# Key path ahead of the queries, squares' low part on GpSimd and the kernel's small constant folded into the context product, in an eight-batch attention and expert kernel

## The reference, cut to what matters

```python
def softmax_kernel(x, proj, is_query):        # 16 heads of 16, proj is 64 x 16
    xp = einsum('bhnd,md->bhnm', x * norm, proj)
    diag = sum(square(x), -1) * 0.5 * norm * norm
    stab = max(xp, -1) if is_query else max(xp, (-1, -2))
    return ratio * (exp(xp - diag - stab) + EPS_K)
qp, kp = softmax_kernel(q, ..., True), softmax_kernel(k, ..., False)
k_sum = sum(kp, 2);  denom = einsum('bhnm,bhm->bhn', qp, k_sum)
ctx = einsum('bhnm,bhnd->bhmd', kp, v)
out = einsum('bhnm,bhmd->bhnd', qp, ctx) / denom
```

## Time and profile before

| | us |
|---|---|
| median of three runs | 785.72 (785.5 to 789.7) |
| the profiled execution's own time | 786.12 |
| its span, first to last instruction | 784.4 |
| TensorE busy | 728.6 (93%) |
| VectorE busy | 619.0 (79%) |
| ScalarE busy | 469.6 (60%) |
| GpSimd busy | 375.3 (48%) |
| mean granted TensorE clock, of full speed | 0.977 |

### The profile page before, as it was taken

One profiled execution on the slowest core, in us unless ns is written; L12 is line 12 of the kernel. 1 busy time (PEld: TensorE's weight loads), 2 busy tenths in 40 slices (PEclk: granted clock), 3 DMA queues, 4 the chain that ended last, 5 costly groups with the idle time before them and its releaser, 6 DMA issues. The chain is left out here.

```text
span 784.4 us, 16225 instructions
## 1 busy us (share of the span) xinstructions
PE 728.6 (93%) x6009; PEld 597.0 (76%) x6009; DVE 619.0 (79%) x1304; ACT 469.6 (60%) x749; POOL 375.3 (48%) x358
## 2 busy tenths in 40 slices
PE   8999999999999999999999979968999999999950
PEld 7867768778778778778778758857888889998850
DVE  5976678888888888888888797888768767778683
ACT  4656747867867867867868834463245544455470
POOL 4364317527527527527617613511347556544563
PEclk9999999999999999999999999999999999999985
DMA  8100010011011011011011011250336664446593
GB/s 252 33 2 2 1 54 2 28 54 57 28 53 54 27 53 54 27 53 54 27 54 29 29 55 54 60 193 2 124 134 163 160 165 112 107 148 168 138 266 112
DMA packets 51184, 62.60 MB, mean 80 GB/s; under 512 B 9408, under 2 KB 44992, under 8 KB 51136
## 3 DMA queue, kind: packets, MB, share of 16 engines
q1 hardware_dynamic: 44016, 49.74, 19.3%
q0 software_dynamic: 6864, 12.19, 7.9%
q10 hardware_dynamic: 256, 0.03, 0.0%
HBM read 40.85 MB, written 21.10 MB: 79 GB/s over the span
## 5 line engine op out<-in xcount | busy, mean ns | idle before, releaser
L2181 PE MATMUL pF<-w,h 128*128 128x256 f32 x448 | 109.8, 386 | 0.0
L2181 PEld LDWEIGHTS pF<-w,h 128*128 128x128 f32 x448 | 80.7, 190 | 17.6 <-issue 8.6
L1139 POOL DMA_INDIRECT kp<-row_scratch,idx_g x32 | 43.3, 1353 | 76.5 <-DVE idx_g L1851 53.5
L904 ACT ACTIVATE h<-pX,b1cur 128x512 f32<-128x512 f32 x64 | 43.9, 689 | 56.4 <-DVE b1cur L1954 41.8
L2636 PE MATMUL pX<-w_lo,h_hi 128*128 128x256 f32 x256 | 73.9, 289 | 0.8 <-issue 0.8
L2636 PE MATMUL pX<-w_hi,h_lo 128*128 128x256 f32 x256 | 72.4, 283 | 0.0
L2636 PE MATMUL pX<-w_hi,h_hi 128*128 128x256 f32 x256 | 72.4, 283 | 0.0
L993 POOL TENSOR_SCALAR ve<-mv 128x4 f32<-128x4 f32 x36 | 8.5, 237 | 133.2 <-DVE mv L1216 132.3
L1147 POOL DMA_INDIRECT acc_scratch<-qp,idx_s x28 | 55.5, 1982 | 21.5 <-DVE qp L1891 16.6
L1912 DVE TENSOR_TENSOR h_lo<-h,h_hi 128x512 fp32r<-128x512 f32 x64 | 42.5, 690 | 22.9 <-ACT h_hi L896 22.2
L1321 DVE RECIPROCAL den<-den 128x512 f32<-128x512 f32 x14 | 46.9, 3348 | 7.9 <-ACT den L551 7.9
(11 more groups left out here) (435 smaller groups left out, 2165.6 us busy)
## 6 DMA issues: line engine op xcount, KB each, us to landing
kp<-fc1T SPq DMA_DIRECT2D x8, 1024.0 KB
w<-fc2T SPq DMA_DIRECT2D x8, 1024.0 KB
xin<-video SPq DMA_DIRECT2D x7, 512.0 KB, 3.5
x<-video SPq DMA_DIRECT2D x7, 512.0 KB, 4.5
out<-x SPq DMA_DIRECT2D x7, 512.0 KB, 3.0
acc_scratch<-xf SPq DMA_DIRECT2D x7, 512.0 KB, 2.9
row_scratch<-y SPq DMA_DIRECT2D x7, 512.0 KB, 3.0
kp<-acc_scratch SPq DMA_DIRECT2D x4, 512.0 KB, 5.8
```

Source lines behind the costliest of these rows:

```text
L904: nc.scalar.activation(h[:, n, :], pM[n % M_SLOTS], ACT.Gelu_apprx_tanh, bias=b1cur[:, n:n + 1]).then_inc(he_ready, 1)
L1139: pool.indirect_dma_start(xg[:, g, :], None, row_d, bass.IndirectOffsetOnAxis(ap=idx_g[:, g:g + 1], axis=0)).then_inc(first_rows[g] if isi ...
L2181: ins = nc.tensor.matmul(pF[m][:, half * D:(half + 1) * D], h[:, k, tok(2 * m + half)], w2[:, k, :], start=(k == 0), stop=(k == FC - 1))
```

## The change

It does the following.

- **Order on TensorE, batches 2 to 7:** `key_features(0)` goes ahead of the values, `key_features(1)` ahead of the first `hidden`; `turn_kmax` comes after three `hidden` steps (before: six), `spread_kmax` after five (before: seven), the second query features after six (before: seven). `ff_out` is handed out in counts: 2, turn_tops, 6, context, features_turned(0), 4, sums_of_keys, features_turned(1), turn_context, 4, all_heads, 5, transposes of xf, 3, gates, 3, turn_x, turn_gates, 5. Batch 1 keeps its early keys and has the same rest.
- **VectorE:** both first `k_max` stand ahead of the low part of x2T, `k_top` ahead of the first two `q_max`; `rest_of_squares` is gone from batches 1 to 7; the statistics of the next batch and `scores` stand ahead of `residual`; `add_ff(0)` behind `sums_of_context`; the gates' copy behind both `heads_out`.
- **ScalarE:** `eps_k` is gone; the exp of the key tiles goes between the last relus, the norms of z behind them, `cs_copy(0)` ahead of `exp_q(0)`; xf's norm behind `dens`; `normed_rows` to the end.
- **GpSimd:** runs `rest_of_squares` behind the two passes over x2; the ksum adds wait for all four `k_sub`; `xnb` goes to the end of the batch.
- **EPS_K:** the key tile gets two more columns of EPS_K behind each pair of 128 (stride 130). `context` multiplies 129 columns, so that the last one is EPS_K times the sum of the values; `cs_copy(0)` copies that column out and adds it as a bias, `cs_copy(1)` adds 512 times EPS_K. The extra products of batch 0 are gone.
- `ones_h` and `sdiag` have 128 rows (before 16). On SyncE the DMA of the scores comes one batch later, behind that of y.

```diff
@@ ScalarE
             def cs_copy(i, n):
                 act.wait_ge(a_ready, i * A_JOBS + J_CTX + n + 1)
-                nc.scalar.activation(cs[:, n, :], pA[n][:, 0:G * P], ACT.Copy).then_inc(cs_ready, 1)
+                if n:
+                    nc.scalar.activation(cs[:, 1, :], pA[1][:, 0:G * P], ACT.Identity, bias=epsn_c[:, 0:1]).then_inc(cs_ready, 1)
+                else:
+                    wide = pA[0][:, 0:G * PW].rearrange("p (g x) -> p g x", x=PW)
+                    nc.scalar.activation(vsum[:].unsqueeze(2), wide[:, :, P:P + 1], ACT.Copy).then_inc(vsum_ready, 1)
+                    act.wait_ge(vsum_ready, i + 1)
+                    for g in range(G):
+                        ins = nc.scalar.activation(cs[:, 0, g * P:(g + 1) * P], wide[:, g, 0:P], ACT.Identity, bias=vsum[:, g:g + 1])
+                    ins.then_inc(cs_ready, 1)
...
-            def eps_k(i, t):
-                act.wait_ge(ke_ready, (i - 1) * TT + t + 1)
-                nc.scalar.activation(kp[:, t, :], kp[:, t, :], ACT.Identity, bias=epsk_c[:, 0:1]).then_inc(kp_ready, 1)
...
@@ GpSimd
+            def rest_of_squares(i):
+
+                pool.wait_ge(qsq_ready, (i + 1) * 2)
+                pool.wait_ge(x_ready, (i - 1) * X_JOBS + J_QT + 2)
+                nc.gpsimd.tensor_tensor(qsq_lo[:], qsqT, qsq_hi[:].bitcast(F32), ALU.subtract).then_inc(ql_ready, 1)
...
+                if is_first(i):
+                    pool.wait_ge(bias_ready, 1)
+                    biased_rows()
+                else:
+                    pool.wait_ge(ks_ready, (i + 1) * TT)
+                    for t in range(1, TT):
                         pool.wait_ge(kp_ready, i * TT + t + 1)
...
+                if not is_first(i):
+                    pool.wait_ge(obias_ready, i + 1)
+                    biased_rows()
...
@@ VectorE
+                k_top(i, sa)
+                q_max(i, 0)
+                q_max(i, 1)
+                dve.wait_ge(dg_ready, (i + 1) * 2)
+                k_shift(i)
+                k_sub(i, 0)
+                k_sub(i, 1)
+                q_max(i, 2)
+                q_max(i, 3)
+                parts_of_tops(i)
+                k_sub(i, 2)
+                k_sub(i, 3)
...
@@ TensorE
+                hidden(0)
+                hidden(1)
+                pe.wait_ge(qT_ready, (i + 1) * G)
+                features(i, J_XQ, qT, 0)
+                hidden(2)
+                turn_kmax()
+                hidden(3)
+                hidden(4)
+                spread_kmax()
+                hidden(5)
+                features(i, J_XQ + 1, qT, 1)
+                hidden(6)
+                hidden(7)
+                ff_out(2)
+                turn_tops()
+                ff_out(6)
+                context()
+                features_turned(0)
+                ff_out(4)
+                sums_of_keys()
+                features_turned(1)
+                turn_context()
+                ff_out(4)
+                all_heads()
+                ff_out(5)
...
```

More of the change, by code:

```diff
@@ L736, in body @@
+                if not is_ahead(i):
                     squares(i, 0)
                     squares(i, 1)
[L738 to L766, removed]
+                key_rows(1)
+                relu(f, 0)
+                relu(f, 1)
@@ new lines, in body @@
+                q_squares(i)
+                for n in range(2, 6):
+                    relu(f, n)
+                exp_k(i, 0)
+                relu(f, 6)
+                exp_k(i, 1)
+                relu(f, 7)
+                q_tops(i)
+                exp_k(i, 2)
+                exp_k(i, 3)
+                if ut:
+                    for t in range(TT):
+                        z_norm(u, t)
+                cs_copy(i, 0)
+                exp_q(i, 0)
+                cs_copy(i, 1)
+                exp_q(i, 1)
@@ L1044, in body, with biased_rows @@
                     shift(0, 1, nx)
[L1046 to L1054, removed]
+                def biased_rows():
                     wait(pool, r_ready, i * 2)
@@ L1436, in body @@
                     normed(1, f, x2, r).then_inc(x2_ready, 1)
[L1437 to L1440, removed]
+                sa = Steps(dve, dve_a, STEPS_A, i)
                 if u is not None:
                     normed(2, u, z, z).then_inc(zn_ready, 1)
[L1443 to L1454, removed]
+                k_max(i, 0)
+                k_max(i, 1)
+                for c in range(C):
+                    dve.wait_ge(x2T_ready, f * C + c + 1)
+                    nc.vector.tensor_tensor(x2T_lo[:, c, :], pF[c][:], x2T_hi[:, c, :].bitcast(F32), ALU.subtract).then_inc(x2l_ready, 1)
+                norms(i, 0, dgk)
+                norms(i, 1, dgk)
+                k_max(i, 2)
+                k_max(i, 3)
+                dve.wait_ge(kmx_ready, (i + 1) * TT)
+                nc.vector.tensor_reduce(kmax[:], mxk[:].rearrange("p t h -> p h t"), AX_X, ALU.max).then_inc(kmax_ready, 1)
                 if u is not None:
@@ L2182, in ff_out @@
                                                start=(k == 0), stop=(k == FC - 1))
-                    if half == 1 and k1 == FC:
-                        ins.then_inc(f_ready, 1)
+                        if half == 1 and k == FC - 1:
+                            ins.then_inc(f_ready, 1)
+                    del products[:count]
                 def by_heads(j, w_, g):
@@ L2453, in body @@
[L2453 to L2467 removed]
+                key_features(1)
```

247 lines of the change are left out of this document (83 added, 164 removed).

## The result

The changed kernel takes **798.62 us** (median of 4 runs, 796.16 to 799.9), the kernel before 786.21 (4 runs, 785.5 to 789.7): the ratio is 1.0148, with a 95% interval of 1.0122 to 1.0173. The profiled execution took 799.2 us, with a span of 797.4, against 786.1 and 784.4. The change makes the kernel 13 us slower in that one.

What follows compares the result with a forecast made beforehand. TensorE's own instructions were taken to set a batch. Five batches +7.5, batch 1 +0.55, batch 7 +1.65 and batch 0 -1.0 gave +8.7 on 786.1: 794.8, or 794.4 us against the median; range 781.5 to 803.

Steps and rivals of the forecast that it cites:

- rival B: In k_top, GpSimd's subtraction of the squares holds VectorE's diagonal: 1.2 us more a batch, 802.8 in all; chance 0.20.
- What the order saves: TensorE, batches 2 to 6: fewer tile shape changes and no aT_lo wait gain 0.4 us a batch.
- The wait for aT_lo: TensorE ahead of attention_out: about 0.2 us in a steady batch, 1.03 in batch 1, goes behind six more products.
- A stay in tiles: TensorE's changes of tile shape: each stay costs about 0.18 us beyond its work; eight instead of nine.
- The key path: Keys to last k_sub: turn_kmax at 18.2 us instead of 22.4, last k_sub at 30.0 instead of 33.05.
- A, the wait for the ksum: TensorE ahead of sums_of_keys waits 1.9 us for GpSimd's adds, batch 59.55, 794.4 in all; chance 0.40.
- rival C: At sums_of_keys the adds end by 36.4, so no new wait, not slower: 782.1 us; chance 0.30.
- No new wait on the row tops: TensorE ahead of sums_of_keys: 0.1 us for small waits on the row tops and the fourth exp.
- The six products behind `all_heads`: TensorE: these products could have hidden the 1.9 us wait ahead of sums_of_keys, but were put behind all_heads.
- The ends: First and last batches: batch 0 -1.0 us, batch 1 +0.55, batch 7 +1.65 with gates ending 9.0 after the heads.
- EPS_K and ScalarE: EPS_K's four additions of 1.15 us a batch leave ScalarE: worth nothing in themselves, since TensorE covers them.
- Behind the batches: After batch 7: the forecast sum has no term for this part.

Runs made afterwards that it cites:

- e5: Changed kernel; squares' subtraction after the diagonal, two products moved ahead of sums_of_keys, last batch's behind the gates, xf's norm ahead of denominators: 782.82 us, ratio 0.9948.
- e2: Changed kernel with GpSimd's subtraction of the squares made to wait until VectorE has built the key maxima's diagonal: 788.59 us, ratio 1.0018.
- e7: Changed kernel with the subtraction of the squares back on VectorE, between k_top and the first two q_max: 792.64 us, ratio 1.0073.
- e1: Changed kernel with four feed-forward products moved from behind all_heads to ahead of sums_of_keys: 794.86 us, ratio 1.0118.
- e3: Changed kernel with the five products behind all_heads moved behind the gates in the last batch alone: 797.72 us, ratio 1.0142.
- e4: Kernel before with the EPS_K part of the change alone, every order as before: 797.36 us, ratio 1.0136.
- e6: Kernel before with the EPS_K part alone, plus GpSimd's adds waiting for all four k_sub: 787.39 us, ratio 1.0008.
- e8: Changed kernel without GpSimd's wait for all four k_sub ahead of the adds: 812.04 us, ratio 1.0311.

## Why the prediction was right, and which of its terms were not

The direction and the range held: 794.4 forecast with 781.5 to 803.0, measured 798.62. The mechanism named first, that the ksum's adds end after TensorE wants them, is there at the forecast place. But the runs give it a much smaller share than it was given, and most of the loss came by rival B. By steps:

**What the order saves.** Forecast 0.4 us a batch. The runs show about 0.75: TensorE's own work is 57.3 in e5, against 58.07 before, and e2 gives the same (58.20 less the 0.85 by which its ksum comes late). The wait for aT_lo is gone from the steady batches. A stay in tiles was priced too low at 0.18: in the earlier trace rows the four instructions from 387.99 to 389.05 take 1.06 where 4 x 0.215 is 0.86, so that a stay costs 0.2 behind it alone. Of the 59.84 us that a batch of the changed kernel takes, about 2.5 are therefore not TensorE's work. Its three waits are 2.07 in the list and some 2.4 by the distance of the starts, since the list counts from the modelled end of the instruction before.

**The key path.** Forecast: kmax turned at 18.2, measured 18.25. The last `k_sub` was forecast at 30.0, with the diagonal as slow as before; measured 30.99 with the hold and 29.35 without it (e2). The prediction's 11.5 us for VectorE's run kept the 0.93 of the earlier trace rows, though the xnb beside which it had been so long was no longer there.

**A, the wait for the ksum.** This is the term that was mis-sized. Forecast were 1.9 us with TensorE's arrival at 36.4, and a batch of 59.55. By itself (e2) the wait is 0.79, or 0.85 by the starts, and the batch 58.20: 1.35 less than forecast, 1.05 of it by the wait and the rest by what the order saves. The arrival was right: 37.34 less 0.85 is 36.5 in e2. The adds were the error: they start at 29.52 in e2, not at 30.05, and `residual` in the middle of them costs 0.5 (two adds in 5.30, not in 4.76), not 0.95. So **rival C's point was nearer than thought**: with B out of the way the result is "the same" (788.59 in e2), where A forecast 794.4.

**B, the hold.** Forecast as a rival with 0.20, at 1.2 us a batch; it happened in batches 1 to 7 (2.12 to 2.21 each time), and costs 1.64 a batch. The 0.3 us on which it hung went the way that makes it slow: the subtraction started at 18.65, the diagonal at 18.87. B moves the start of A's adds, and the prediction rightly put its price on top of A's; A and B together are its 802.8, as far above the measured time as 794.4 is below. What it got wrong is how the loss is shared. A and the savings were to make a batch 1.5 longer, and make it 0.13 longer (e2); B, which is not in the sum of 794.4 at all, makes it 1.64 longer, and the whole kernel about 10 us (798.62 against 788.59). **That 794.4 came within 4.2 us of the result is therefore in good part luck:** A's price, too large by 1.35 a batch, stood in for B's.

**No new wait on the row tops.** The prediction allowed 0.1 for them. They are 0.37 and 0.33, and both hang on B: they are gone in e2, and in e7 from the list, where only about 0.2 of the second is left by the starts.

**The six products behind `all_heads`.** The prediction said that they could have hidden the wait. e1 shows that they can't by themselves: they hide it, and the wait comes back at xf and at the gates' copy. With the key path 1.64 us earlier, two of them are enough (e5).

**The ends.** Batch 1: +0.89 for +0.55. Batch 7: +2.04 for +1.65, with the gates' copy at 9.05 after the heads for a forecast of 9.0. Both hold B, which wasn't in these sums; without it, in e2, they are −0.62 (62.30) and +0.47 (62.91). Batch 0: −0.98 for −1.0. In e3 a longer stretch at 1.2 GHz goes with a batch 0 longer by as much, but the two traces compared here lost about the same to it (0.72 and 0.71 over 33 to 39 us before, 0.66 and 0.78 after). e4 shows the gain too, with no order changed: from the keys of batch 0 to those of batch 1 it takes 40.01 us, the changed kernel 40.03, the kernel before 41.15.

**EPS_K and ScalarE.** Costed at nothing outside batch 0. e6 agrees: 1.0008. But e4 shows the cover on which this rests: only with the wait for all four `k_sub` is it nothing; alone, the shorter exp path costs 1.4%. The prediction took that wait for a cost only, with what was queued behind it, and didn't ask what it keeps apart.

**Behind the batches.** Nothing was forecast there and +2.0 us came. They are there by the experts' first matmul (587.5 against 574.8). The windows of the changed kernel from 560 to 580 us:

```profile
560.00:570.00 10.00, 9.79 (x69) 9.00 (x68) 7.64 (x12) 0.00 (x0) 5.11 (x4) 0.82 0.21 56
570.00:580.00 10.00, 10.00 (x49) 8.42 (x48) 5.39 (x13) 4.13 (x7) 1.21 (x1) 0.67 0.64 236
```

and the same work in the kernel before:

```profile
550.00:560.00 10.00, 9.83 (x71) 9.39 (x70) 7.47 (x13) 0.37 (x1) 5.13 (x4) 0.83 0.19 54
560.00:570.00 10.00, 10.00 (x56) 8.40 (x54) 7.95 (x15) 6.09 (x11) 3.43 (x2) 1.00 0.68 243
```

The clock has two levels, 2.4 and 1.2 GHz: a granted 0.82 and 0.67 are 10.2 us at 1.2 GHz, which leave out (0.18 + 0.33) x 10 = 5.1 us of full clock, against 1.7 before. Another 1.7 were missing before from 500 to 520 us (granted 0.94 and 0.89), but there TensorE was busy for 8.87 and 7.01 us of 10 and lost less by it. This is enough for the two microseconds, and the experts' matmuls behind take 180.1 us in both. In both traces a stretch in which TensorE pauses often (busy 5.9 to 7.2 of 10 us) and then about 16 us at 9.8 to 9.9 of 10 lie ahead of the fall. The other traces tell whether the change has a part in it. From the first step of the last hidden layer to the experts' first matmul it takes 108.43 to 108.50 us in the three whose last 25 us there were granted 0.80 (the changed kernel, e2 and e4), and 105.88 to 107.78 in the seven with 0.86 or 0.93. Among those seven are the kernel before with 106.50, and e1 and e5, which have the changed order, with 106.41 and 106.04. So the two microseconds go with the granted clock and not with the change; what decides how long it stays at 1.2 GHz there isn't known. The unchanged kernel's own runs go from 785.28 us at a mean clock of 0.979 to 790.07 at 0.972.

## What to carry to other kernels

Look at what a small VectorE instruction on the critical path has beside it on GpSimd: if GpSimd's large operation starts a few tenths earlier, the small one lasts as long as the large one, and one wait that lets it go first (e2) can be worth as much as the whole change loses. A wait that seems to make a chain late may be keeping two engines apart, and an addend taken out of a chain can cost time by starting the next step sooner (e4, e8); so when a change shortens a path, list what will now run beside what. And where several mechanisms lie on one path, check each one's price by an experiment of its own, even when the sum comes out: here the total was near, and the shares of the hold and of the late ksum were not.

## What the runs showed of the hardware

Where VectorE's instruction is held, it is held to the end. Over four places the length of the held VectorE instruction is what was left of GpSimd's: 0.93 in the earlier trace rows, 1.55 (e4), 2.06 (e8), 2.21 (the change), and each ended within 0.05 us of the GpSimd operation; with no such GpSimd operation begun before it, each took 0.20 or 0.22. These are tiny instructions (16x16 and 128x64); that the conversion of the row tops would be held like the diagonal I had not expected. Not every small VectorE instruction is held: the four statistics of x that start at 391.62 in the changed kernel, inside the third add, take 1.40 together, as they do elsewhere (a single one 0.39 to 0.43 over the whole run), and a sum of the gates' numbers (0.15, at 387.44) and its reciprocal (0.18, at 387.62) begin and end inside the first add.

The Trainium skill, SBUF — State Buffer, section "SBUF: two separate sides", says that VectorE and GpSimd share a pair of ports as an exclusive lock, for VectorE's operations in a two-port mode or with two inputs in SBUF, and that whoever starts first keeps it for the whole instruction. The trace agrees, with 375.77 against 375.75 us for the two ends in batch 6.
